# The scatter of a decoder layer's routed rows: eight indirect DMAs in a row, or four pairs, each behind a product of TensorE

## What is computed

```python
x = x + attn(_layernorm(x), Wq, bq, ...)
x = x + xattn(_layernorm(x), ctx_2048, wq, ...)        # qdq on the queries' input and on the output
x = x + ffn(_layernorm(x), router_w, w_gate, w_up, w_down)

# in ffn
topk_w, topk_idx = jax.lax.top_k(softmax(xf @ router_w.T), 8)
pos = position of the pair (token, expert) among the pairs of its expert, in order of tokens
valid = pos < 128
buf = zeros((64 * 128 + 1, h)).at[dest].set(xf[slot_token])      # dest = expert * 128 + pos, or nowhere
hmid = silu(xb @ w_gate) * (xb @ w_up);  yb = hmid @ w_down
out = zeros((T, h)).at[slot_token].add(yb[dest] * topk_w)
```

## Time and profile before

| | |
|---|---|
| median of three runs | 1680.09 us |
| the profiled execution | 1680.71 us, of which its span is 1678.9 us |
| turns 6 to 35 (first scatter to last that the change touches) | 162.8 to 1234.5 us of the span |
| the experts' half | from about 1285 us on |
| busy share of the span | PE 85%, DVE 71%, ACT 56%, POOL 43% |

### The profile page before, as it was taken

How to read it: one execution, slowest core, us unless ns; L and a number is a source line. 1 busy time by engine, 2 the same in 40 slices (tenths; PEclk the granted TensorE clock), 3 DMA queues, 4 the chain that set the end, 5 groups by cost and what they waited for, 6 DMA issues and landing times.

```text
span 1678.9 us, 36380 instructions
## 1 busy us (share of the span) xinstructions
PE 1421.1 (85%) x11243; PEld 1069.3 (64%) x11276; DVE 1189.6 (71%) x3054; ACT 940.6 (56%) x3309; POOL 727.1 (43%) x718
## 2 busy tenths in 40 slices
PE   5499889999988999889899999989864888888895
PEld 3377667777666777666677777767643655555564
DVE  3778878888887888888788888888862444444453
ACT  2367676676666666666666766666742333333342
POOL 1113434444443444445444344444433454445565
PEclk8699999999999999999999999999976999999997
DMA  6765322222211111111111001110464999999964
GB/s 187 296 220 205 136 94 100 92 92 95 100 46 36 38 32 31 31 56 32 31 38 31 31 31 56 31 31 26 161 227 153 282 280 276 279 263 282 280 103 52
DMA packets 164530, 204.33 MB, mean 122 GB/s; under 512 B 40246, under 2 KB 122422, under 8 KB 164481
## 3 DMA queue, kind: packets, MB, share of 16 engines
q1 hardware_dynamic: 125568, 165.86, 30.0%
q0 software_dynamic: 38912, 37.87, 11.1%
HBM read 136.19 MB, written 130.29 MB: 159 GB/s over the span
## 4 chain that ended last, share of the span: by engine, by line
PE 37%; DMA 19%; issue 12%; ACT 10%; DVE 8%; another core or an unknown queue 7%; POOL 1%; POOLq 0%; DVEq 0%; SPq 0%
DMA out<-x,slots 19%; PE bank L528 18%; ACT probs L1028 7%; PE bank L556 6%; PE bank L510 3%; PE bank L563 3%; PE bank L534 2%; PE bank L549 2%; PE bank L569 1%; ACT wide_b L1124 1%; ACT wide_b L1099 1%; DVE small L1308 1%; DVE small L1341 1%; POOL routed L1867 1%
## 5 line engine op out<-in xcount | busy, mean ns | idle before, releaser
L1028 ACT ACTIVATE probs<-bank,small 128x128 f32<-128x128 f32 x1024 | 363.5, 389 | 88.1 <-issue 50.0
L1867 POOL DMA_INDIRECT routed<-row,slots x248 | 253.7, 1023 | 126.7 <-issue 77.4
L1822 POOL TENSOR_TENSOR small<-small,half 128x1 f32<-128x1 f32 x96 | 54.4, 567 | 544.5 <-DVE small L1313 544.5
L1950 POOL DMA_INDIRECT out<-x,slots x128 | 199.0, 1554 | 195.8 <-DMA out<-x,slots 148.4
L1022 ACT ACTIVATE probsT<-bank 128x512 f32<-128x512 f32 x254 | 144.2, 609 | 214.4 <-remote 116.3
L1028 ACT ACTIVATION_READ_ACCUMULATOR probs<-bank,small 128x1 f32 x1024 | 234.6, 229 | 0.0
L1341 DVE TENSOR_REDUCE small<-bank 128x4 f32<-128x512 f32 x256 | 166.4, 682 | 23.0 <-PE bank L549 17.6
L556 PE MATMUL bank<-idf,probs 128*128 128x128 f32 x1024 | 164.8, 300 | 8.5 <-ACT probs L1028 8.4
L556 PEld LDWEIGHTS bank<-idf,probs 128*128 128x128 f32 x1024 | 134.1, 156 | 42.0 <-ACT probs L1028 13.2
L1777 DVE TENSOR_SCALAR slots<-pairs 128x1 uint32<-128x1 f32 x128 | 13.7, 149 | 184.0 <-DMA out<-x,slots 180.3
L1271 ACT ACTIVATE xn<-bank 128x192 f32<-128x192 f32 x64 | 21.3, 333 | 148.2 <-PE bank L968 133.0
(11 more groups left out here) (250 smaller groups left out, 3974.5 us busy)
## 6 DMA issues: line engine op xcount, KB each, us to landing
w_gate_up<-in_w_gate SPq DMA_DIRECT2D x128, 192.0 KB
w_gate_up<-in_w_up SPq DMA_DIRECT2D x128, 192.0 KB
w_down<-in_w_down SPq DMA_DIRECT2D x128, 192.0 KB
routed<-empty_row SPq DMA_DIRECT2D x16, 1280.0 KB, 11.3
x_in<-in_x SPq DMA_DIRECT2D x32, 256.0 KB
xn<-in_xT_in SPq DMA_DIRECT2D x32, 256.0 KB
ctx_sb<-in_ctxT_in SPq DMA_DIRECT2D x32, 256.0 KB
x_res<-in_x SPq DMA_DIRECT2D x32, 256.0 KB
```

The lines of the kernel that those rows point to most:

```text
L1028: last = act.activation(probs[:, g, j * P:(j + 1) * P], bank[:, b, j * P:(j + 1) * P], ACT.Exp, bias=negated[:, h:h + 1], **({"accum_out": ...
L1822: pool.tensor_tensor(c["r0"], c["v"], half[:, :], ALU.pow).then_inc(g_pow[kind], 1)
L1867: pool.indirect_dma_start(routed, bass.IndirectOffsetOnAxis(ap=slots_of(m)[:, k:k + 1], axis=0), row_of(m)[:, :], None, bounds_check=SLOTS ...
L1950: pool.indirect_dma_start(out.rearrange("b p (h c) -> (b p h) c", h=2), bass.IndirectOffsetOnAxis(ap=place_of[k % 2][:, half_:half_ + 1], ...
```

## The change

The one call of `scatter` in GpSimd's turn becomes four calls of two DMAs each. The first pair leaves as before when `slots` is there. The second also waits for the first piece of the queries' product of tile `cur - 1` (`queries_a`), the third for the cross queries' product of tile `cur - 3` (`cross_queries`), the fourth for the third set of turned probabilities of tile `cur - 2` (`turn_probs_0`, the second of the two sets that stand behind `cross_output`).

```diff
                 if has(cur - 1):
                     self_power(cur - 1)
                 if has(cur - 5):
-                    scatter(cur - 5)
+                    scatter(cur - 5, 0, 2)
+                if has(cur - 5):
+                    reached(pool, p_q, cur - 1, 3, 1)
+                    scatter(cur - 5, 2, 4)
+                if has(cur - 5):
+                    reached(pool, p_cq, cur - 3, 1, 1)
+                    scatter(cur - 5, 4, 6)
+                if has(cur - 5):
+                    reached(pool, p_pT, cur - 2, 4, 3)
+                    scatter(cur - 5, 6, TOPK)
                 if has(cur - 4):
                     ffn_power(cur - 4)
```

## The result

The change took 1703.76 us (median of 4 runs, 1696.57 to 1704.84) against 1679.26 us (1677.44 to 1685.43) for the kernel before on the same chip: ratio 1.013, 95% interval 1.0092 to 1.0169. The forecast was 1592 us with a range to 1660. It was wrong in its sign.

The account below looks back on a forecast made before the run. No engine was full; TensorE's results, delayed during scatter rows, were taken as the bound. Terms -4.17 + 0.6 + 0.3 = -3.27 us a turn, times 27 = 88 us off the profiled 1680.71, gave 1592 us; range 1560 to 1660.

Parts of the forecast that it names:

- The hold: TensorE's results reach ScalarE and VectorE late while GpSimd issues a row of scatters; removing this gives -4.17 us a turn.
- The row of four: Second and third pair run as one row of four scatters, still delaying TensorE's results somewhat: +0.6 us a turn.
- The depth: How many scatters in a row delay results: those becoming ready within the first four were taken to pass.
- the sign of turn 34: Evidence against pairs: behind only two scatters VectorE began its scores late, at 1194.02, having waited 1.29 us.
- the rival with 0.17: Pairs still delay the cross scores, to 0.44 us behind the fourth pair: 1.8 us a turn gained, 1633 us; chance 0.17.
- The fourth pair: Its new wait makes GpSimd's L1822 finish about when VectorE's L1318 needs it: cost 0 to 0.3, taken as +0.3 us a turn.
- an upper end of 1.4 us a turn: Bound on `number_tokens` and `ffn_normed` waiting for the last pair's landing if GpSimd's slack were gone; costed at nothing.
- The slower rival: Row of four delays everything until its end, then cross scores come 1.4 us behind the fourth pair: 1737 us; chance 0.10.

Follow-up runs that it names:

- the wait in front of the train: Changed kernel, GpSimd's L1877 and what follows also waiting for VectorE's L1322: 1546.71 us, 0.9937 on the first chip; 1577.60 us, 0.9437 on the third.
- eight in a row: Kernel before, scatters uncut, with only the added wait that holds GpSimd's L1877 until VectorE's L1322 is done: 1670.20 us, 0.9997 on the third chip.
- fours: Kernel before with the scatters cut into two calls of four, plus the wait of L1877 for VectorE's L1322: 1603.55 us, 0.9605 on the third chip.
- the broken train after a rest: Changed kernel with GpSimd also waiting for the eighth scatter's landing ahead of `ffn_power` (L1822): 1605.78 us, 1.0313 on the second chip.
- the five powers: Kernel before plus, behind its eight scatters, the change's fourth wait and five small unread GpSimd powers: 1681.24 us, 1.005 on the third chip.

## Why the prediction was wrong

**The hold, -4.17 us a turn: right in kind.** "Remote" is all but gone from L1022, the wait before L1384 fell from 96.1 to 30.1 us in after and to 15.5 with the wait in front of the train (the loop's list of waits of that kernel), and with that wait the clock went to 1.00 (0.97 in after). With the train out of the way the gain on the third chip was 93.7 us (1671.29 - 1577.60); I had worked out 88, and 33 to 34 us for a turn, which is 33.17. From eight in a row to pairs, both with the wait, a turn gave 3.26 us; my sum was 3.27. The reading of the two turns in the earlier trace rows held. On the two chips without the hold before is 117 to 125 us faster, which sizes the stall from another side, if the chips differ in nothing else: I had put all of it at 27 x 4.17 = 113.

**The row of four, +0.6: right.** With the pairs and the wait VectorE still waits 15.5 us before L1384, 0.6 a turn, and mostly begins there 1.1 to 1.2 us behind the end of the row; with fours 25.4 us are held at another copy.

**The depth: wrong.** I concluded that what becomes ready within the first scatters of a row passes. It does not always: behind a pair the cross scores come 0.33 to 0.48 us after its end. That was the sign of turn 34 and the rival with 0.17. It costs VectorE 13.0 us in the loop with the wait, 0.5 a turn, for which the sum had no term.

**The fourth pair, +0.3: the step that failed.** I asked when L1822 would be done and when VectorE needed it, found them level, and that was right: L1318 follows on L1822 without a long wait in after (512.62 behind 512.30). Then I named `bias_residual`, `ctx_hi` and `ctx_lo` as queued behind it and gave them no term at all; `number_tokens` and `ffn_normed` I costed "at nothing", since GpSimd "has its slack afterwards". I had asked only who waits for their results. What they cost is the place where they run: ready in a block behind a scatter, they shut out VectorE's next instruction with two SBUF inputs. That was +3.24 us a turn (3.52 against 0.28), 78.8 us in the loop's list, in place of zero. Put together from different chips: the pairs with the wait gain 93.7 us on the third, and leaving the wait out costs 107.2 from the first to the second (1653.95 - 1546.71), which makes +13.5. The measured sum is +24.5 us. The other 11 were not isolated; VectorE's waits before L1384 and L1341 are 23.7 us longer in after's loop than with the wait (52.2 against 28.5), and TensorE's L556 now waits 53.1 us for L1379, in the chain behind L1322.

**The bounds.** The term had an upper end of 1.4 us a turn, from a landing. The trace of before held the true one, 3.13 us for L1322 in the one turn where GpSimd was late. A group's mean (263 ns) hid it; the spread of the line's durations shows it. The slower rival (0.10) had the right sign, and that is luck: it asked for a row of four that still holds all until its end and for scores 1.4 us behind the fourth pair. The scores are held, but for 0.3 to 0.5 us behind a pair, and the loss came from VectorE's L1322, which no rival names.

**The rule that was weighed.** I set the trace against the Trainium skill's rule that engines do not block one another without a semaphore, for the held results. The row that mattered lay elsewhere. L1322 lasts to the end of L1877 in the turn of before that is shown, and for the train in after. The Trainium skill has this in "SBUF — State Buffer", section "SBUF: two separate sides": GpSimd and a VectorE instruction with two SBUF inputs lock one pair of ports for a whole instruction, and the second blocks. The trace agrees for one instruction (L1322 lasts up to 1.24 us in the usual turns of before, 0.16 where nothing is in its way). The section does not say that several instructions, here four, can hold as one, which is the 3.5 us. The Trainium skill's "GPSIMD Engine Reference", section "2.1 Instruction dispatch", warns that consecutive instructions are no barrier between GpSimd's cores, each of which goes on by itself. If a scatter leaves the cores out of step, some core would always be inside a tensor instruction until the queue is empty, which would fit the broken train after a rest and the unbroken one behind the five powers. This is argued, not shown: no trace here sees single cores. Against its last part speaks L1843, which follows the train without a gap (516.57) and yet lets L1322 in ahead of it.

**What stays open.** Why results were held in the first comparison and on the third chip (before at 1679 and 1671 us) and not on the first and second (1554) no run here can tell. The hold's own mechanism is as unknown as at the start, and so is why a rest of GpSimd breaks the train. The change itself ran on the chip of the first comparison and on the second, the pairs with the wait on the first and third, so their ratios are each to before on another chip.

## What to carry to other kernels

Before making a queue late, list everything that stands ready behind the delayed instruction and ask what runs beside it, not only who waits for it. In this kernel GpSimd's tensor instructions, when it had not rested since its last scatter, shut out VectorE's two-SBUF-input instructions until the end of L1836. A wait that lets VectorE's instruction go first cost nothing (0.9997 with eight in a row) and took the pairs from 1.013 to 0.944 of before where results are held, and from 1.065 to 0.994 where they are not. And look for the odd turn in the trace of before: the one in which the queue happened to be late is the experiment, already run.

## What the runs showed of the hardware

- A 128x1 product on VectorE took 0.16 us free, up to 1.24 us against one GpSimd instruction, 3.5 to 3.8 us in most turns against a train of four tensor instructions when GpSimd had not rested since a scatter; L1338, L1368 and L1371, with an input in TensorE's banks, kept their 0.68 us inside such a train.
- The same kernel took 1679 us in the first comparison, 1671 on the third chip and 1554 on the first and second, with the runs of each chip within 0.8%. Where it takes 1554, the "remote" waits behind the rows of scatters are absent.
- Where results are held, even two scatters hold them: the cross scores reached VectorE 0.33 to 0.48 us behind the end of a pair, up to 1.4 us after TensorE was through.
- GpSimd paused among its scatters twice in the kernel before, with 113 scatters from one pause to the other; the first was 4.10 us long, one in the kernel with the powers 5.91 (before the scatter at 1192.00). In the kernels whose GpSimd is otherwise early with L1822, the one or two turns of 3.1 to 3.8 us came behind such a pause.
